# Scores of 64 context keys by one full 32-bit product in place of three split terms

## The reference

```python
q1, k1, v1 = x @ Wq1, x @ Wk1, x @ Wv1      # from x, 512 positions, split into 8 heads of 64
k2, v2 = ctx @ Wk2, ctx @ Wv2               # from the context, 64 positions
k, v = concatenate([k1, k2], 1), concatenate([v1, v2], 1)      # 576 keys
attn = softmax(einsum('bihd,bjhd->bhij', q1, k) * scale)
out = einsum('bhij,bjhd->bihd', attn, v).reshape(b, 512, 512) @ Wo + bo
```

## Time and profile before

| | |
|---|---|
| median of 3 runs | 4375.89 us |
| profiled execution | 4397.46 us |
| its span, first to last instruction | 4395.7 us |
| TensorE busy, whole span | 3439.4 us (78%) |
| VectorE busy | 2820.9 us (64%) |
| ScalarE busy | 2073.9 us (47%) |
| mean granted clock of TensorE | 0.898 |

### The profile page before, as it was taken

How to read it: one execution, slowest core, us unless ns; L and a number is a source line. 1 busy time by engine, 2 the same in 40 slices (tenths; PEclk the granted TensorE clock), 3 DMA queues, 4 the chain that set the end, 5 groups by cost and what they waited for, 6 DMA issues and landing times. The chain is left out here.

```text
span 4395.7 us, 81705 instructions
## 1 busy us (share of the span) xinstructions
PE 3439.4 (78%) x25420; PEld 2507.5 (57%) x25421; DVE 2820.9 (64%) x7262; ACT 2073.9 (47%) x4994; POOL 1385.9 (32%) x1108
## 2 busy tenths in 40 slices
PE   5878788758689588888888879999998409999970
PEld 3555555537678356666556556777767306666650
DVE  5888888868867488888888846666666311121116
ACT  4777777753242165555555536555555101111110
POOL 1333333324300376666665702122222350000004
PEclk9999999988799799999899989999999559999995
DMA  2000000010010211111111110000000720010013
GB/s 68 6 7 7 7 7 7 1 34 19 25 74 1 66 44 35 30 44 37 35 40 31 33 41 7 11 6 6 6 1 1 242 80 27 29 31 29 29 35 105
DMA packets 101919, 147.71 MB, mean 34 GB/s; under 512 B 19904, under 2 KB 71552, under 8 KB 100800
## 3 DMA queue, kind: packets, MB, share of 16 engines
q1 hardware_dynamic: 95424, 126.58, 9.5%
q0 software_dynamic: 6144, 16.79, 1.2%
HBM read 61.52 MB, written 31.46 MB: 21 GB/s over the span
## 5 line engine op out<-in xcount | busy, mean ns | idle before, releaser
L1012 DVE TENSOR_SCALAR a_t<-a_t,a_inv 128x512 f32<-128x512 f32 (+3 forms) x768 | 719.1, 979 | 9.0
L695 PE MATMUL a_T<-ident,a_t 128*128 128x128 f32 x3328 | 535.3, 300 | 163.8 <-DVE a_t L1012 89.8
L854 ACT ACTIVATE a_t<-a_t,a_neg 128x512 f32<-128x512 f32 (+3 forms) x1024 | 642.5, 634 | 7.7 <-DVE a_neg L1040 7.3
L845 ACT ACTIVATE a_pT<-a_T 128x512 f32<-128x512 f32 (+3 forms) x1024 | 484.7, 514 | 328.1 <-PE a_T L695 324.6
L695 PEld LDWEIGHTS a_T<-ident,a_t 128*128 128x128 f32 x3328 | 402.7, 151 | 379.8 <-issue 217.0
L884 POOL TENSOR_TENSOR a_t<-a_t,a_inv 128x512 f32<-128x512 f32 x256 | 284.4, 1133 | 653.5 <-DVE a_inv L1008 653.5
L1035 DVE CUSTOM_DVE_ANT_0 a_t<-a_A,a_decay 128x512 f32<-128x512 f32 x512 | 322.7, 685 | 91.0 <-PE a_A L655 89.3
L884 POOL TENSOR_TENSOR x_t<-x_t,x_inv 128x576 f32<-128x576 f32 x128 | 158.1, 1257 | 696.3 <-DVE x_inv L1008 696.3
L2096 DVE COPY experts_y<-experts_Y 128x256 f32<-128x256 f32 x72 | 30.6, 425 | 513.9 <-PE experts_Y L2034 513.9
L909 POOL TENSOR_TENSOR a_rsin<-a_rawswapped,a_sin 128x512 f32<-128x512 f32 x128 | 170.1, 1329 | 583.5 <-DMA a_rawswapped<-a_raw 558.7
L1035 DVE CUSTOM_DVE_ANT_0 a_t<-a_A,a_table 128x384 f32<-128x384 f32 (+3 forms) x512 | 224.1, 485 | 128.5 <-PE a_A L667 125.6
(11 more groups left out here) (273 smaller groups left out, 7243.1 us busy)
## 6 DMA issues: line engine op xcount, KB each, us to landing
a_rawswapped<-a_raw SPq DMA_DIRECT2D x512, 64.0 KB, 2.0
ex_w<-in_f_w_dram SPq DMA_DIRECT2D x16, 1024.0 KB, 13.6
moe_sent<-route_zeros SPq DMA_DIRECT2D x1, 9216.0 KB, 29.5
experts_xg<-moe_sent SPq DMA_DIRECT2D x72, 128.0 KB, 2.0
moe_results<-experts_y SPq DMA_DIRECT2D x72, 128.0 KB, 1.7
a_xin<-x_all SPq DMA_DIRECT2D x16, 512.0 KB, 4.1
x_xin<-x_all SPq DMA_DIRECT2D x16, 512.0 KB, 2.9
x_all<-in_x_dram SPq DMA_DIRECT2D x1, 4096.0 KB, 14.9
```

The costliest lines, as they stand in the source:

```text
L695: mm = pe.transpose(bank[:, kt, :], t_of(u, j, kt * P, (kt + 1) * P), sh.ident[:])
L845: nc.scalar.activation(to, of, ACT.Copy).then_inc(t_empty, 1)
L854: nc.scalar.activation(t_of(u_e % U, j, 0, n), t_of(u_e % U, j, 0, n), ACT.Exp, bias=neg[:, slot, j:j + 1], scale=SCALE, accum_out=total[: ...
L1012: nc.vector.tensor_scalar(t_of(u_n % U, j, 0, m), t_of(u_n % U, j, 0, m), inv[:, u_n % 4, j:j + 1], None, ALU.mult).then_inc(normed, 1)
```

## The change

k_ctx becomes F32, not F32R, and loses its split into high and low: it holds one copy of the keys, written by VectorE alone (tensor_copy in place of the subtraction). ScalarE's four copies of item 4 (L799) are gone, and with them item 4's wait on hi. A new tile q_raw, 128 x 2 x 2 x 512 of F32, holds q unsplit; ScalarE writes it by a second copy of the same bank right behind the high part of items 0 and 1. The scores of the 64 keys are then one F32 product for each pair, two a step in place of six. The scores of the 512 other keys are computed as before, from q_hl and k_hl. HI_GROUP goes from 8 to 6, HI_ITEM counts the new order: VectorE's low part of items 0 and 1 now waits for both copies, as both read the bank that it frees.

```diff
--- before.py
+++ after.py
@@ -320,10 +320,10 @@
     T_JOBS = U * T_UNIT
     T_CREDIT = 4 * T_UNIT
     N_O = 2 if a0 else 2 * G
-    HI_GROUP = {"a0": 2, "a1": 4, "x1": 8}[kind]
+    HI_GROUP = {"a0": 2, "a1": 4, "x1": 6}[kind]
     LOW_GROUP = {"a0": 4, "a1": 4, "x1": 0}[kind]
 
-    HI_ITEM = (1, 2, 3, 4, 8)
+    HI_ITEM = (2, 4, 5, 6) if x1 else (1, 2)
 
     with ExitStack() as ctx:
         env = Env(nc, ctx, kind)
@@ -386,7 +386,8 @@
             rest = sb("rest", [P, S])
             rsin = sb("rsin", [P, S])
         if x1:
-            k_ctx = sb("kctx", [P, 2, 2, 4, SC], F32R)
+            k_ctx = sb("kctx", [P, 2, 4, SC])
+            q_raw = sb("qraw", [P, 2, 2, S])
             v2 = sb("v2", [SC, IN])
             ctxT = sb("ctxT", [P, DT, SC])
             wk1 = sb("wk1", [P, DT, IN])
@@ -673,9 +674,8 @@
                     pe.wait_ge(*seg.empty(turn, name))
                     bank = A[seg.bank(name)]
                     for pr in range(2):
-                        for n, (ql, kl_) in enumerate(((0, 1), (1, 0), (0, 0))):
-                            mm = pe.matmul(bank[:, 2 * pr * SC:2 * (pr + 1) * SC], q_hl[:, gp, ql, pr, q],
-                                           k_ctx[:, gp, kl_, 2 * pr:2 * pr + 2, :], start=(n == 0), stop=(n == 2))
+                        mm = pe.matmul(bank[:, 2 * pr * SC:2 * (pr + 1) * SC], q_raw[:, gp, pr, q],
+                                       k_ctx[:, gp, 2 * pr:2 * pr + 2, :], start=True, stop=True)
                     mm.then_inc(a_full, 1)
 
             def transpose_head(b, ug, u, j):
@@ -790,14 +790,9 @@
                     act.wait_ge(*seg.full(turn, name))
                     if i < 2:
                         nc.scalar.activation(q_hl[:, gp, 0, i, :], bank[:], ACT.Copy).then_inc(hi, 1)
+                        nc.scalar.activation(q_raw[:, gp, i, :], bank[:], ACT.Copy).then_inc(hi, 1)
                     elif i < 4:
                         nc.scalar.activation(k_hl[:, gp, 0, i - 2, 0:S], bank[:], ACT.Copy).then_inc(hi, 1)
-                    else:
-                        for pr in range(2):
-                            for half in range(2):
-                                r = slice(64 * half, 64 * half + 64)
-                                nc.scalar.activation(k_ctx[r, gp, 0, 2 * pr + half, :],
-                                                     bank[r, pr * SC:(pr + 1) * SC], ACT.Copy).then_inc(hi, 1)
 
             def raw_copy(seg, turn, b, work):
                 _, g, i = work
@@ -822,7 +817,7 @@
                     to, of = (v2[:, col], bank[0:SC, 0:V_CUT]) if x1 and i == 2 else \
                         (v_sb[:, 2 * i:2 * i + 2, col], bank[:].rearrange("p (k n) -> p k n", k=2))
                     nc.scalar.activation(to, of, ACT.Copy).then_inc(v_done, 1)
-                elif work[0] == "item":
+                elif work[0] == "item" and work[2] < 4:
                     high_parts(seg, turn, b, work[1], work[2])
 
             def step(seg, turn, b, s, prev, own, nxt):
@@ -933,7 +928,7 @@
                 if a1:
                     nc.vector.memset(scratch[:], 0.0).then_inc(ready, 1)
                 if x1:
-                    nc.vector.memset(k_ctx[:].bitcast(F32), 0.0).then_inc(ready, 1)
+                    nc.vector.memset(k_ctx[:], 0.0).then_inc(ready, 1)
                     nc.vector.memset(table[:], 0.0).then_inc(ready, 1)
                 dve.wait_ge(ready, N_READY)
                 dve.wait_ge(weights, 16 * len(loads))
@@ -962,7 +957,8 @@
                     name = ("item", g, i)
                     bank = A[seg.bank(name)]
                     dve.wait_ge(*seg.full(turn, name))
-                    dve.wait_ge(hi, b * HI_GROUP * G + (HI_GROUP * g + HI_ITEM[i]))
+                    if i < 4:
+                        dve.wait_ge(hi, b * HI_GROUP * G + (HI_GROUP * g + HI_ITEM[i]))
                     if i < 2:
                         ins = nc.vector.tensor_tensor(q_hl[:, gp, 1, i, :], bank[:], q_hl[:, gp, 0, i, :], ALU.subtract)
                     elif i < 4:
@@ -973,8 +969,7 @@
                             for half in range(2):
                                 r = slice(64 * half, 64 * half + 64)
                                 h = 2 * pr + half
-                                ins = nc.vector.tensor_tensor(k_ctx[r, gp, 1, h, :], bank[r, pr * SC:(pr + 1) * SC],
-                                                              k_ctx[r, gp, 0, h, :], ALU.subtract)
+                                ins = nc.vector.tensor_copy(k_ctx[r, gp, h, :], bank[r, pr * SC:(pr + 1) * SC])
                     ins.then_inc(q_low, 1)
 
             def run(seg, turn, b, work):
```

## The result

The change makes the kernel slower. The kernel after takes 4389.97 us (median of 10 runs, 4384.49 to 4393.74), the kernel before 4378.45 on the same chip (10 runs, 4374.21 to 4381.42): ratio 1.0025, 95% interval [1.0015, 1.0035]. The forecast was 4356.9 us, a ratio of 0.9957. Ratios leave out executions in a slower state, of which there was one in all the runs of this document (18237.64 us, in the kernel with six products).

A forecast was written before the change was run, and what follows sets the result against it. TensorE was taken as the bound, busy 558.5 of 600 us. Score block -12.5, ScalarE's dropped copies -7.1 and q copies +0.6 made -19.0 us, from a median of 4375.89 to 4356.9; range 4346 to 4371.

The forecast's parts named there:

- The step that failed: TensorE's queue in the second cross attention: work leaving it leaves the span, except where waits for ScalarE or VectorE follow.
- The score block: L677 in 64 steps: 0.82 us becomes 0.59, 0.224 off a step; 14.3 us less, 12.5 after losses in steps 6 and 0.
- Step 6 to 7: L667 waits for VectorE's layer norm (L1026) in step 6, so the faster product's 7 x 0.224 = 1.6 us is lost.
- The rival by passes: L677: a full 32-bit product costs its four passes, block 1.09 us, kernel +8.9 us to 4385; chance 0.08.
- the one that took 0.15 us off as well: Between L677 and L716: the 0.15 us at the change of tiles goes too, 8.5 us more, 4348; chance 0.08.
- ScalarE's copies: Without L799 the last transposes (L698) start 0.47 us sooner in 15 steps with item 4: 7.1 us less.
- The copies of q: 32 added ScalarE copies like L792: hidden except in the stage's first step, where TensorE waits +0.6 us.
- The clock: Step 6: the wait grows from 1.3 to 1.5 us and the clock falls, 12.5 us come back, 4369.5; chance 0.10.
- The falls in step 4: Clock falls at L630 after TensorE's 1.93 us wait, costing 1.8 us, may come more or less often: +-4 us.
- two signs of being wrong: L677's loads spaced above 0.15 us, or TensorE waiting anew for VectorE in steps 0 or 2.

The follow-up runs named there:

- six products: Changed kernel with 48 instructions of waits ahead of TensorE's loop and the 64 keys' scores by six F32R products again: ratio to kernel before 0.9979, stage 832.1 us.
- after + 16: Changed kernel with 16 more instructions of already satisfied waits in TensorE's queue ahead of the loop: ratio to kernel before 0.9949, stage 825.6 us.
- copies back: Changed kernel with 48 instructions of waits ahead of TensorE's loop and ScalarE's four item 4 copies restored as dead work: ratio to kernel before 0.9987, stage 838.7 us.
- before + 48: Kernel before with 48 more instructions of already satisfied waits in TensorE's queue ahead of the loop: ratio to kernel before 1.0006, stage 844.7 us.
- after + 200: Changed kernel with 200 more instructions of already satisfied waits in TensorE's queue ahead of the loop: ratio to kernel before 1.0003, stage 845.6 us.
- 272: Changed kernel with 272 more instructions of already satisfied waits in TensorE's queue ahead of the loop: ratio to kernel before 0.9999, stage 842.9 us.
- 160: Kernel before with 160 more instructions of already satisfied waits in TensorE's queue ahead of the loop: ratio to kernel before 1.0068, stage 872.8 us.

## Why the prediction was wrong

**The step that failed** is "Everything else on its queue runs back to back, so what leaves that queue leaves the span". It counts the time of TensorE's instructions and nothing of where they lie: the jump back, which takes none of its own in the sum, was put at no change. By taking 32 instructions out ahead of the loop and 32 out of it, the change moved the jump's target by 32, across a block's start, from 20 instructions behind one to 12 ahead of it, and the list of a turn went from seven blocks to eight. Step 7 to 0 costs 22.6 to 23.2 us for 15.83, 35 us over five jumps: 26.4 idle, less the 0.58 of waiting for VectorE that it covers each time, which leaves 23.5. The other 12 I put down to the lower clock: at the jump shown, the transposes and the four matmuls behind them take 5.24 us for 3.07. Against a gain of 20.5 without the stall, and 1.7 for one fall of the clock less in step 4, that makes +13; the stage shows +12.9, the runs +11.5. The run with 16 instructions more shows that it is the place: it computes the same and is 0.5% faster than the kernel before.

**Could it have been seen?** The size not, the danger yes. The trace of before has the same row in the self attention of layer 0, whose loop is longer (2136 instructions), between 200 and 1150 us, with 68 packets of q8:

```profile
PE a_T L695 <- issue: 16.9, 5, 4.0
```

Five idles, one to a jump. VectorE has five of them in this very stage before the change, and the earlier trace rows showed one, "2.82 us of nothing" at the loop's edge:

```profile
DVE x_inv L1008 <- issue: 14.4, 5, 3.0
```

That asked why TensorE, in the same loop, is free of them, and how near it is to losing that. (What VectorE's are is not shown; they stay with 16 instructions more on TensorE.) The count of packets alone doesn't tell of a stall: between 1750 and 2590 us, in the self attention of layer 1, the trace of before has 53 packets of q8 and no such idle on TensorE; its L695 waits 56.3 us for VectorE there.

**The score block.** Forecast 0.59 to 0.60 us from the first load of L677 to L716's; the timeline of after has 0.65, with the loads 0.11 apart as forecast:

```profile
3022.04 0.53 PEld L677 LDWEIGHTS x_A<-x_kctx,x_qraw 128*128 128x128 f32 x4
3022.69 1.73 PEld L716 LDWEIGHTS x_O<-x_pT,x_v 128*64 128x64 f32 x32
```

After the last load 0.32 us pass, where before it was 0.26. The saving is 0.17 to 0.18 a step and not 0.224. The steps show it in seven of eight (six products against after + 16), 1.24 us a batch, 9.9 in eight; forecast 12.5. Step 6 to 7 gains none, as forecast: VectorE's L1026 takes it. The group has its 256 records:

```profile
L677 PE MATMUL x_A<-x_kctx,x_qraw 128*128 128x128 f32 x256 | 39.1, 275 | 0.0
```

The rival by passes, 1.09 us for the block, is refuted, though its forecast for the kernel (+8.9) came close to the +11.5 measured, by luck; the one that took 0.15 us off as well (0.45) is refuted too. The prediction took the 0.15 over unchanged from fp32r products: it was 0.21 behind full ones.

**ScalarE's copies.** Forecast 0.47 in fifteen steps, 7.1. The steps show 0.53 in step 1 to 2 and 0.83 in step 6 to 7 (copies back against after + 16), 1.36 a batch and 9.2 in the stage (fourteen steps: the first batch's step 1 to 2 gains nothing). Of the 0.83, 0.30 is VectorE's: L667 waits for L1026 1.31 us before and 1.01 with six products, because an idle of 0.21 us marked issue between two of VectorE's L1026 is gone. The 12.2 by stages holds falls of the clock as well. L698 in a step with item 4, in after + 16:

```profile
3101.43 0.60 PE L701 MATMUL x_T<-ident,x_t 128*64 128x128 f32 x4 [0.34 <-ACT x_pT L843]
```

**The copies of q** cost 0.5 us in the first step and nothing after, as forecast (0.6). VectorE waits for them in step 5, 2.29 us for 1.80, and it is hidden. L972 takes 220 ns for the 0.22 forecast. The wait from the timeline, the two groups from the list of after:

```profile
2961.43 0.69 DVE L963 TENSOR_TENSOR x_qhl<-x_A,x_qhl 128x512 fp32r<-128x512 f32 x1 [2.29 <-ACT x_qraw L793]
```
```profile
L793 ACT ACTIVATE x_qraw<-x_A 128x512 f32<-128x512 f32 x32 | 18.9, 591 | 0.0
L972 DVE COPY x_kctx<-x_A 64x64 f32<-64x64 f32 x64 | 14.1, 220 | 0.7
```

**The clock.** The rival had step 6's wait grow from 1.3 to 1.5 us and the clock fall behind it. In the steady batches of after the wait shrank to 1.2 and the step took 9.65 us throughout, so its condition was not met. The kernel with the copies back met it: L672 waits 1.48 us there, and in two of six batches the step takes 12.07 us for 10.48 (start, duration; then the window). Without the copies of q, behind a wait of 1.36 us, it fell in two of six as well.

```profile
3073.21 1.52 PE L672 MATMUL x_A<-x_khl,x_qhl 64*128 64x512 f32 x6 [1.48 <-DVE x_mx L1031]
```
```profile
3073.00:3077.00 4.00, 3.79 (x19) 3.05 (x19) 3.65 (x14) 0.93 (x2) 0.31 (x1) 0.57 0.01 2
```

In the last batch, where the wait is 2.37 us, it came in after as well (11.73 us for 10.57 before), but also in before + 48 (11.69), so it can't be put down to the change. The falls in step 4 cost 6.7 us less in the steady batches of after and 1.7 more in the last, -5.0 where 4 either way was allowed for.

So the terms were -9.9, -9.2 and +0.5, -18.6 for the -19.0 forecast; that the sum agrees is luck, as the first was too large and the second too small by nearly the same. With the falls of the clock the stage of after + 16 is 20.5 us shorter. The forecast holds for the change without the stall, which is not what was to be predicted. A chance of 0.08 for slower, all of it on one rival about the product's price, left no room for a cost that lies in no instruction. Neither of its two signs of being wrong came: L677's loads were 0.11 us apart, and TensorE waited for VectorE nowhere anew in steps 0 or 2.

## What to carry to other kernels

Where a loop runs without fetching its instructions, its length in blocks is a resource: before an edit of TensorE's list, even a shortening one ahead of the loop, look whether a loop in the trace has idles marked issue behind its jump, on any engine, and how many packets the instruction queue moved in it; after it, look again before reading anything else. If the idle is new, move the loop by some instructions that hide under an existing wait and measure again: here 16 turned +0.25% into -0.5%. And compare step by step: the sum of the gains came out right here while one term was a quarter too large and the other a quarter too small.

## What the runs showed of the hardware

- TensorE repeated a loop of at most seven blocks of 256 instructions with 6 to 8 packets in six turns, and fetched one that touched eight with 43 or 51, at idles of 2.2 to 4.0 us, one or two at a jump (one jump of after + 200 had none); the place of the loop decides, with a period of 256 (16 and 272 alike). That q8 is TensorE's queue is inferred.
- After such an idle its next matmuls ran partly at the lower clock (3.20 us for 1.98), so the idle costs more than itself: 7.1 us for 5.3 on average.
- Two full 32-bit products of 128 columns cost 0.65 us where six fp32r products of this size cost 0.82: the loads kept 0.11 us, 0.06 was added behind the last.
- Waits already satisfied cost TensorE's queue 0.108 us an instruction (two waits each) where nothing hides them: 25.8, 30.1 and 37.9 us idle with 160, 200 and 272.
- Behind a wait of 1.48 us the clock fell in two of six batches (0.57 of full speed over the 4 us with it), at a cost of 1.6 us, and so it did behind one of 1.36 us; behind waits of 1.01, 1.19 and 1.31 us at the same place it fell in none of six.
